# First stage and first layer norm five tiles ahead instead of three, and two steps without a first stage

## What is computed

```python
x = _layernorm(x + einsum('bsi,oi->bso', x, W + delta_W))       # first stage and first layer norm
z = x @ ternary_quant(W_syn).T + b_syn                          # 512 -> 2048
k = max(1, int(2048 * (1.0 - 0.9)))                             # 204
thresh = top_k(z, k)[-1]                                        # the 204th largest of each row
hidden = where(z >= thresh, relu(z), 0.0)
out = hidden @ ternary_quant(W_out).T + b_out                   # 2048 -> 512
x = layernorm(x + out) * gamma + beta
x = _layernorm(x)
```

## Time and profile before

| | us |
|---|---|
| median of 3 runs | 633.76 (633.39 to 636.13) |
| the profiled execution, its own time | 634.05 |
| span of its trace, first to last instruction | 632.3 |
| PE busy in the span | 586.0 |
| ACT busy | 544.0 |
| DVE busy | 539.4 |
| POOL busy | 376.3 |

### The profile page before, as it was taken

The page is one execution under the profiler, slowest core; times in us unless marked ns, Lnnn a source line. Parts: engine busy times, 40 slices in busy tenths (PEclk is TensorE's granted clock), DMA queues, the critical chain, the costliest instruction groups (busy, mean ns, idle before and its releaser), DMA issues.

```text
span 632.3 us, 8712 instructions
## 1 busy us (share of the span) xinstructions
PE 586.0 (93%) x2482; PEld 266.3 (42%) x2482; DVE 539.4 (85%) x657; ACT 544.0 (86%) x724; POOL 376.3 (60%) x712
## 2 busy tenths in 40 slices
PE   8799669999999999999999999999999999997573
PEld 7434324444444444444444444444444444443221
DVE  5796998998998899888888888898998888899882
ACT  1797659999999999999999999999999999989942
POOL 0126386777776547585565457545857555757773
PEclk9999789999999999999999999999999999999887
DMA  8982234545465454555454554545564454434462
GB/s 331 320 263 51 50 83 85 116 91 129 100 109 126 66 118 87 113 101 133 95 124 100 103 117 73 123 78 125 102 133 90 95 101 100 79 74 83 91 95 80
DMA packets 184581, 71.66 MB, mean 113 GB/s; under 512 B 168144, under 2 KB 176336, under 8 KB 183888
## 3 DMA queue, kind: packets, MB, share of 16 engines
q1 hardware_dynamic: 184528, 71.07, 51.2%
HBM read 20.72 MB, written 8.39 MB: 46 GB/s over the span
## 4 chain that ended last, share of the span: by engine, by line
PE 71%; DVE 8%; issue 6%; POOL 6%; ACT 3%; DMA 1%; DVEq 0%; POOLq 0%; ACTq 0%
PE z_ps L972 27%; PE o_ps L992 15%; PE u_ps L955 14%; PE o_ps L985 14%; ACT junk L542 2%; DVE w_sb L772 1%; DVE w_sb L815 1%; DVE z_sb L801 1%; POOL tmp L423 1%; DVE m L777 1%; POOL nmean L374 1%; POOL b L388 1%; ACT hh L579 1%; DVE hT L751 1%; POOL rs L384 1%
## 5 line engine op out<-in xcount | busy, mean ns | idle before, releaser
L542 ACT ACTIVATE junk<-z_sb,t_col 128x2048 f16<-128x2048 f32 x128 | 255.1, 1995 | 10.8 <-POOL t_col L442 9.8
L972 PE MATMUL z_ps<-t_syn,xhT 128*128 128x512 f16 x1024 | 231.0, 379 | 2.7 <-DVE t_syn L663 2.7
L972 PEld LDWEIGHTS z_ps<-t_syn,xhT 128*128 128x128 f16 x1024 | 99.8, 98 | 134.3 <-issue 18.1
L985 PE MATMUL o_ps<-t_out,hT 128*128 128x512 f16 x512 | 122.4, 395 | 16.8 <-DMA hT<-hh 12.4
L955 PE MATMUL u_ps<-weff,xT_sb 128*128 128x512 f32 x256 | 117.5, 602 | 2.3 <-ACT x1s L561 2.3
L992 PE MATMUL o_ps<-t_out,hT 128*128 128x512 f16 x512 | 116.1, 380 | 0.0
L423 POOL TENSOR_SCALAR tmp<-signs,dev 128x1 f32<-128x1 f32 x64 | 40.3, 629 | 124.3 <-ACT junk L542 123.4
L801 DVE SCALAR_TENSOR_TENSOR z_sb<-z_ps,sc,bias_z 128x1024 f32<-128x1024 f32 x64 | 82.0, 1280 | 18.4 <-PE z_ps L972 18.2
L772 DVE SCALAR_TENSOR_TENSOR w_sb<-z_sb,t_col 128x2048 f32<-128x2048 f32 x32 | 86.6, 2707 | 6.4 <-POOL t_col L442 6.2
L542 ACT ACTIVATE junk<-z_sb,start 128x2048 f16<-128x2048 f32 x32 | 64.0, 2001 | 29.7 <-DVE z_sb L801 29.7
L985 PEld LDWEIGHTS o_ps<-t_out,hT 128*128 128x128 f16 x512 | 51.5, 101 | 83.1 <-issue 16.0
(11 more groups left out here) (118 smaller groups left out, 605.4 us busy)
## 6 DMA issues: line engine op xcount, KB each, us to landing
xT_sb<-in_xT SPq DMA_DIRECT2D x16, 512.0 KB, 4.0
out_y<-y_sb SPq DMA_DIRECT2D x32, 256.0 KB, 2.9
z_sb<-in_w_synT SPq DMA_DIRECT2D x4, 1024.0 KB, 12.3
hh<-in_w_outT SPq DMA_DIRECT2D x2, 1024.0 KB, 9.6
z_sb<-in_w_outT SPq DMA_DIRECT2D x2, 1024.0 KB, 10.5
hT<-hh SPq DMA_TRANSPOSE x66, 4.3
weff<-in_wT SPq DMA_DIRECT2D x2, 512.0 KB, 4.7
w_sb<-in_dwT SPq DMA_DIRECT2D x2, 512.0 KB, 5.6
```

The costliest lines, as they stand in the source:

```text
L542: a_.activation(junk[:, n % 2, :], z_sb[:, t % ZS, :], ACT.Sign, bias=at, scale=-1.0, accum_out=signs[:, j, r:r + 1]).then_inc(counted, 1)
L972: last = mm(z_ps[:, c, b * BANK:(b + 1) * BANK], xhT[:, j, h * KD + k, :], t_syn[:, k, n0:n0 + BANK], start=k == 0 and h == 0, stop=k == K ...
L985: mm(o_ps[t % OS][:, :], hT[:, j, 0, c, :], t_out[:, c, :], start=c == 0, stop=False)
```

## The change

`mm1`, `square1`, `scales` and `ln1_out` run five tiles ahead of `mm2` instead of three from step 5 on. Two more first stages are therefore done in the fill. At steps 12 and 20 there is none, so the lead is five up to step 11, four from step 12 and three from step 20 on. `hi_x` stays three tiles ahead. `x1s` has ten buffers instead of eight. The order of the fill and of the drain is written out. The core of the diff (the constant names in the calls of the fill are numbers now):

```diff
-A_X, A_LN1, A_MM1 = 1, 3, 3
+SKIPS = (12, 20)
+A_X, A_HI, A_LN1, A_MM1 = 1, 3, 5, 5
...
-ZS, XS, OS = 6, 8, 3
+ZS, XS, OS = 6, 10, 3
...
+FILLED, DRAIN = 5, 28
...
+def first_of(s):
+
+    return s + A_LN1 - sum(s >= k for k in SKIPS)
...
             for s in range(FILLED, DRAIN):
...
+                if s not in SKIPS:
+                    square1(s, first_of(s))
+                first_step(s)
...
+                if s not in SKIPS:
+                    ln1_out(s, first_of(s))
+                hi_h(s - 1)
+                count(s, 3)
+                hi_x(s + A_HI)
...
+            for s in range(FILLED, DRAIN):
+                mm2(s, 0)
+                mm3_hi(s - L_MM3)
+                flags(s - L_SEL)
+                mm3_lo(s - L_MM3)
+                mm2(s, 1)
+                if s not in SKIPS:
+                    mm1(first_of(s))
```

More of the change, by code:

```diff
@@ L594, in _ @@
             sum_nnz()
[L595 to L596 removed]
+            sign_syn(5)
+            sign_syn(6)
+            sign_syn(7)
             sum_out(0)
[L598 removed]
+            square1(-3, 2)
             sum_out(1)
@@ new lines, in _ @@
+            count(1, 0)
+            square1(-1, 4)
+            first_step(1)
+            count(1, 1)
+            second_step(1)
+            count(0, 4)
+            count(1, 2)
+            ln1_out(-1, 4)
+            square1(0, 5)
+            ln1_out(0, 5)
+            hi_h(0)
+            square1(1, 6)
+            count(1, 3)
+            ln1_out(1, 6)
+            hi_x(4)
+            count(2, 0)
+            square1(2, 7)
+            first_step(2)
+            count(1, 4)
+            count(2, 1)
@@ new lines, in _ @@
+            second_step(2)
+            count(2, 2)
+            ln1_out(2, 7)
+            hi_h(1)
+            count(2, 3)
+            hi_x(5)
+            count(3, 0)
+            square2(3, 0)
+            square1(3, 8)
+            first_step(3)
+            count(2, 4)
+            count(3, 1)
+            second_step(3)
+            count(3, 2)
+            ln1_out(3, 8)
+            hi_h(2)
+            count(3, 3)
+            hi_x(6)
+            square3(4, 0)
+            count(4, 0)
@@ new lines, in _ @@
+            count(28, 0)
+            square2(28, 25)
+            square1(28, 31)
+            first_step(28)
+            count(27, 4)
+            count(28, 1)
+            second_step(28)
+            count(28, 2)
+            ln1_out(28, 31)
+            hi_h(27)
+            count(28, 3)
+            hi_x(31)
+            square3(29, 25)
+            ln3_out(28, 24)
+            count(29, 0)
+            square2(29, 26)
+            first_step(29)
+            count(28, 4)
+            count(29, 1)
@@ new lines, in _ @@
+            below(26)
+            top8(26)
+            lo_x(29)
+            select(26)
+            centre(24)
+            hidden(26)
+            general(26)
+            add_v(28, 24)
+            evac(28, 0)
+            lo_h(26)
+            evac(28, 1)
+            add_r(25)
+            below(27)
+            top8(27)
+            lo_x(30)
+            select(27)
+            centre(25)
+            hidden(27)
+            general(27)
+            add_v(29, 25)
+            evac(29, 0)
@@ new lines, in _ @@
+            lo_h(27)
+            evac(29, 1)
+            add_r(26)
+            below(28)
+            top8(28)
+            lo_x(31)
+            select(28)
+            centre(26)
+            hidden(28)
+            general(28)
+            add_v(30, 26)
+            evac(30, 0)
+            lo_h(28)
+            evac(30, 1)
+            add_r(27)
+            below(29)
+            top8(29)
+            select(29)
+            centre(27)
+            hidden(29)
+            general(29)
+            add_v(31, 27)
@@ new lines, in _ @@
+            evac(31, 0)
+            lo_h(29)
+            evac(31, 1)
+            add_r(28)
+            below(30)
+            top8(30)
+            select(30)
+            centre(28)
+            hidden(30)
+            general(30)
+            add_v(32, 28)
+            lo_h(30)
+            add_r(29)
+            below(31)
+            top8(31)
+            select(31)
+            centre(29)
+            hidden(31)
+            general(31)
+            add_v(33, 29)
+            lo_h(31)
```

448 lines of the change are left out of this document (316 added, 132 removed).

## The result

The changed kernel took 637.2 us (median of 19 runs, 633.99 to 639.98) against 633.52 us for the kernel before (20 runs on the same chip). A twentieth run took 1034.43 us at a mean granted clock of 0.557, the slow state of the chip, and is left out. The ratio is 1.005, with a 95% interval from 1.0038 to 1.0062: slower by half a per cent, clear of the noise. The medians are 3.7 us apart, more than the 3.2 us that I had called no change. The profiled execution took 636.92 us with a span of 635.1 us, 2.8 us more than before.

The account below looks back on a forecast made before the run. PE bounds the steady steps, a chain over ACT, POOL and DVE the fill. 634.05 + 4.4 (fill) - 3.8 (short steps) = 634.65 us for the profiled execution, 634.5 said; range 630.8 to 637.6.

Parts of the forecast that it names:

- The short steps: Steps 12 and 20 without a first stage: PE gains 1.63 and 2.14 us until it waits for `ok`, together 3.8.
- The chain in the fill: Fill: `square1(7)` waits for `mm1(7)`, so `count(1,4)` starts at 90.7 and `hi_h(1)` at 97.9, 3.3 us later.
- The clock: Fill, `mm1(6)` after 2.8 us of idle PE: 1.5 us added for the low clock.
- 0.4 off for `mm1(5)`: Fill: `mm1(5)` begins after a shorter idle time than before, so 0.4 us was taken off.
- The hand-over to `mm1(6)`: Fill, `mm1(5)` to `mm1(6)`: `square1(5)` 0.8, `scales(0)` 1.3, `ln1_out(5)` 0.67 us; `mm1(6)` starts at 75.5.
- The drain: End of the kernel: predicted to stay as before.
- My upper bound of the fill, 5.4 us: Fill: both first stages at the low clock, 3.3 + 2.1 = 5.4 us later.
- Rival 3: Fill: clock low before `mm1(5)` and `mm1(6)`, `mm2(3,0)` slow too; 7.1 us in the fill, 637.4 us; chance 0.14.
- rival 1: Fill swallows both stages, for instance with `mm1(5)` at full clock and no slow `mm1(6)`: price 1 us or less, 630.8; chance 0.13.
- rival 2: Steps 12 and 20: the full 3.44 us come back at each, 631.6 us; chance 0.08.
- rival 4: Steps 12 and 20 give nothing, as another wait stands right behind `flags`: 638.4 us; chance 0.05.
- The Trainium skill: Fill: by its page the 1.5 us may vary between executions, so the fill costs between 4.4 and 2.9 us.

Follow-up runs that it names:

- the clock held: Changed kernel plus matmuls without use, 18 before `mm1(5)` and 12 before `mm1(6)`: 632.87 us against 634.51 for the kernel before, ratio 0.997.
- one moved operation: Changed kernel with the matmuls without use, and `square1` of tile 7 behind `count(2,1)`: 630.48 us (ratio 0.9941), on another chip 632.02 us (0.996), against the kernel before.
- once more: The changed kernel itself, unedited, run again on another chip: 636.18 us against 633.75 for the kernel before, ratio 1.004; its profiled execution took 633.46 us.
- `square1(7)` later: Changed kernel with only `square1` of tile 7 moved behind `count(1,4)` and `count(2,1)`: 633.89 us against 634.51 for the kernel before, ratio 0.9987.
- short steps 12 and 13: Changed kernel with the two steps without a first stage at 12 and 13 instead of 12 and 20: 638.95 us, one run.
- short steps 5 and 6: Changed kernel with the two steps without a first stage at 5 and 6 instead of 12 and 20: 639.32 us against 634.51 for the kernel before, ratio 1.0064.
- clock held, once more: Second trace of the changed kernel with matmuls without use before `mm1(5)` and `mm1(6)`, on another chip: 630.82 us, one run.
- one ahead: Changed kernel with lead four, only step 12 without a first stage, `mm1(6)` before `mm3_hi(0)`: 635.05 us against 634.34 for the kernel before, ratio 1.0006.

## Why the prediction was right, and where it was short

I said 634.65 us for the profiled execution and no change; it was 636.92, and the medians, 637.2 against 633.52, differ by 0.6%. The time lies inside my range of 630.8 to 637.6, near its upper end, but also just above the 636.9 from which I had called it slower, which I had given 0.17. `flags(3)` at 130.37 is later than the 128 to 129 that I had named and short of the 131 at which I would have called the prediction wrong.

- **The short steps: right.** 1.63 + 2.14 = 3.8 us predicted from where `ok` stood, 1.73 + 2.10 measured, with waits of 1.63 and 1.26 us (1.3 to 1.9 named). The gain was partly lost again only where such steps followed each other or the fill.
- **The chain in the fill: right.** It is `square1(6)`, `square1(7)`, `count(1,4)`, `hi_h(1)`, `lo_h(1)`. In the execution in which `mm1(6)` ran at the full clock, `count(1,4)` started at 90.50 (90.7 predicted), `hi_h(1)` at 97.60 (97.9) and `flags(3)` 2.98 us later than before (2.9 for that case). That it fits so closely is partly luck: `mm1(5)` took 5.37 us there and ended 0.5 us earlier than I had it, which hid the hand-over behind it, 0.6 too short in my sum.
- **The clock: mis-sized.** "1.5 us are added" for `mm1(6)` was the wrong term. I took it from a row of `mm3_hi` that lost 1.5 us after 2.40 us of idle time; here `mm1(6)` lost 2.77 us (6.37 against 3.60), since it ran almost wholly at the low clock; with the clock held both `mm1` took 3.67 us and `flags(3)` came 5.0 us earlier. I also took 0.4 off for `mm1(5)`, which ended at 72.60, as the row of the old order would have it: 0.4 short. With 1.3 for `mm1(6)`, this is 1.7 us.
- **The hand-over to `mm1(6)`: 0.6 short.** From the end of `mm1(5)` to `mm1(6)` I had 2.9 us; it was 3.5, in both traces of this kernel. POOL's power in `scales(0)` took 1.41 us beside DVE, not the 0.89 of the earlier trace rows. These terms make 2.3 us; the chain behind `mm1(6)` was 0.5 shorter than I had it, which leaves the 1.8 us between 4.4 and 6.2. The drain adds 0.3, where I had said that it stays as before.
- **My upper bound of the fill, 5.4 us, was broken.** 6.2 was measured, and 6.5 and 6.6 in the two traces with the short steps elsewhere. I had added 2.1 us for a second `mm1` like the one of 5.73 us, as if that row were the worst case; at 6.37 us a `mm1` loses 2.8.
- **Rival 3 came half true.** It gave 637.4, close to the median of 637.2, with the clock low for both `mm1`; but `mm2(3)` did not run slowly (7.07 us with its tail, as before), so its 7.1 us in the fill were 6.2. I gave it 0.14 because less idle time stands ahead of `mm1(6)` than in the rows I had. The 3.3 us that do stand there had a slow `mm1(6)` behind them in three traces with this fill and a fast one in two. Given that and the spread of the 31 runs, both levels deserved a chance near one half, and the forecast would have been their middle or the worse one.
- **Rivals 1, 2 and 4 fell.** `square1(7)` did not fit ahead of POOL's guess (with the clock held, which was rival 1's own condition, the fill still cost 1.2 us, near the 1 us that it named), the short steps gave 3.8 and not 6.9, and they did not give nothing.
- **The Trainium skill** (TensorE: Matmul & The Clock Gate, "What's actually happening") says that the throttled phase is not tied to the kernel's start and so varies from run to run. The two traces of the changed kernel agree: 6.37 and 3.67 us for the same matmuls after 3.32 and 3.31 us. I had worked out 2.9 to 4.4 us in the fill by it. The lower end was seen at 2.98; the upper was too low for the reason above.

The chain was right; the clock's price was the term that was off most, the hand-over and the drain were short by less, and "no change" came out as slower by a little. What the working missed is that the price is not one number: the fill costs 3.0 us in one execution and 6.2 in the next, against 3.8 us given back.

## What to carry to other kernels

Work put into an engine's idle time is free only if nobody on the path waits for it, in the queue of every engine that it passes; here one small activation ahead of a long count passed PE's delay on to the whole fill. A stage left out in the steady part gives what the next wait leaves, so read the reserve of the operation that is waited for, and space such steps until it has grown again. Where a matmul on the path follows idle time, count it at both clock levels, and try filler matmuls there: they turned this change from 1.005 of the time before to 0.997 (0.996 and 0.9941 together with one moved operation, whose own share is 0.5 us of the fill), and did nothing for the time where no one was waiting.

## What the hardware showed that I had not expected

- **The same idle time gives either clock.** After 3.31 or 3.32 us of idle PE `mm1(6)` took 3.67 us in two traces (once more, `square1(7)` later) and 6.37, 6.38 and 6.48 in three (changed, short steps 12 and 13, short steps 5 and 6). In the two `mm1(5)` had taken 5.37 and 5.74 us, in the three 5.94, 5.97 and 6.17: where the clock came back later, it fell again before `mm1(6)`. Five traces are few for a rule. Ahead of the last `mm3_hi`, 3.25 us of waiting were followed by 3.61 us of work and 3.75 by 5.30, but in the once more profiled changed kernel 2.40 us were followed by 5.29. Waits at `flags` of up to 1.85 us never had a slow matmul behind them. A wait of 1.86 us had 5.31 us behind it in one trace (clock held, once more) and 3.63 in another (one ahead). Of the eleven waits from 2.69 to 3.31 us nine had a slow matmul behind them.
- **An earlier PE can be a slower one.** In two kernels the wait at `flags(1)` grew to 3.14 and 3.31 us mostly because PE came sooner, and the matmuls behind it took 5.23 and 6.35 us instead of 3.63. The place of the low clock moves with the schedule.
- **POOL's power on 128x3 elements has no fixed price.** It takes 0.88 us by itself and was recorded at 2.96 us in the changed kernel, beside DVE's back-to-back operations on 2048 columns:

```profile
83.57 2.96 POOL L435 TENSOR_TENSOR rs<-var,cst 128x3 f32<-128x3 f32 x1
```

With the clock held it stood at 3.36 us, at another place of DVE's queue. It delays the guess of tile 1, which is what `count(1,4)` waits for once `square1(7)` is out of its way (0.27 us with that edit alone, 0.94 with the clock held too).
